# History sums of a chunked delta-rule recurrence: a transfer within SBUF in place of a round trip through DRAM, and another placement of the history products

## The reference, cut to what matters

```python
def step(St, inp):                 # one of 128 steps, for 16 sequences x 16 heads
    kt, qt, vt, at, bt = inp
    Sk = jnp.einsum('bhij,bhj->bhi', St, kt)
    err = Sk - vt
    Sn = at[..., None] * St - (bt[..., None] * err)[..., None] * kt[:, :, None, :]
    ot = jnp.einsum('bhij,bhj->bhi', Sn, qt)
    return (Sn, ot)
```

## Time and profile before

| what | value |
| --- | --- |
| median of 3 runs | 3042.21 us (3035.08 to 3061.76) |
| the profiled execution's own time | 3051.64 us |
| its span | 3050.0 us |
| TensorE, VectorE, ScalarE, GpSimd busy | 68%, 61%, 35%, 39% of the span |
| the recurrence, leaves 0 to 15 | 681.6 to about 1919 us, 1237 us |

### The profile page before, as it was taken

One profiled execution on the slowest core, in us unless ns is written; L12 is line 12 of the kernel. 1 busy time (PEld: TensorE's weight loads), 2 busy tenths in 40 slices (PEclk: granted clock), 3 DMA queues, 4 the chain that ended last, 5 costly groups with the idle time before them and its releaser, 6 DMA issues. The chain is left out here.

```text
span 3050.0 us, 41308 instructions
## 1 busy us (share of the span) xinstructions
PE 2080.3 (68%) x12114; PEld 1426.5 (47%) x12114; DVE 1852.3 (61%) x4462; ACT 1056.3 (35%) x2356; POOL 1183.0 (39%) x1443
## 2 busy tenths in 40 slices
PE   8999999966766666556556446599967553479700
PEld 4555555534555554444345335578733331157600
DVE  5777777767776677776667548545537482023234
ACT  2555555534444444444334234222300100112200
POOL 1444444446443333333333323244444217311175
PEclk8999999987787787787777777799989565579955
DMA  3666666663677788999999993422221602048732
GB/s 93 121 121 121 120 121 121 121 148 71 155 189 176 198 210 222 232 243 240 245 241 251 263 281 82 155 76 76 77 83 33 218 11 71 1 144 264 219 101 84
DMA packets 680751, 457.64 MB, mean 150 GB/s; under 512 B 309583, under 2 KB 625790, under 8 KB 674312
## 3 DMA queue, kind: packets, MB, share of 16 engines
q1 hardware_dynamic: 550891, 314.96, 40.9%
q0 software_dynamic: 50080, 96.70, 11.8%
q10 hardware_dynamic: 79616, 44.06, 5.0%
HBM read 245.54 MB, written 207.77 MB: 149 GB/s over the span
## 5 line engine op out<-in xcount | busy, mean ns | idle before, releaser
L918 ACT ACTIVATE p_diag_o<-p_ident,p_gd 128x128 f32<-128x128 f32 x1152 | 361.7, 389 | 509.2 <-PE p_ps_o L874 483.2
L384 DVE SCALAR_TENSOR_TENSOR p_y<-p_ps_proj,p_w,p_y 128x508 f32<-128x508 f32 (+2 forms) x576 | 416.0, 741 | 115.4 <-ACT p_y L298 101.8
L874 PE MATMUL p_ps_o<-p_ws,p_diag_o 128*128 128x128 f32 x1792 | 327.3, 340 | 128.4 <-DVE p_ws L620 80.0
L726 POOL DMA_DIRECT2D p_near_g<-gram x512 | 284.5, 565 | 289.3 <-PE p_ps_n L847 288.8
L874 PEld LDWEIGHTS p_ps_o<-p_ws,p_diag_o 128*128 128x128 f32 x1792 | 284.0, 240 | 200.6 <-DVE p_ws L620 101.8
L833 PE MATMUL p_ps_z<-p_turned,p_gcol 112*32 112x128 f32 x3584 | 159.6, 319 | 318.3 <-DMA p_turned<-history 318.2
L234 PE MATMUL p_ps_proj<-p_x,p_w 128*128 128x512 f32 x768 | 343.1, 597 | 2.7 <-ACT p_beta_t L289 2.7
L198 POOL TENSOR_TENSOR p_kq<-p_y,p_sig 128x512 f32<-128x512 f32 x128 | 162.2, 1271 | 377.6 <-ACT p_sig L309 376.9
L833 PEld LDWEIGHTS p_ps_z<-p_turned,p_gcol 112*32 112x32 f32 x3584 | 104.7, 126 | 382.4 <-DMA p_turned<-history 343.0
L570 DVE SCALAR_TENSOR_TENSOR p_zo<-p_ws,p_gd,p_zo 128x128 f32<-128x128 f32 x768 | 243.9, 351 | 3.8
L564 DVE TENSOR_TENSOR p_ws<-p_ws,p_dec 128x128 f32<-128x128 f32 (+2 forms) x192 | 119.0, 620 | 205.7 <-PE p_ps_o L874 205.7
(11 more groups left out here) (223 smaller groups left out, 3837.0 us busy)
## 6 DMA issues: line engine op xcount, KB each, us to landing
history<-p_hist SPq DMA_DIRECT2D x18, 2048.0 KB, 14.9
gram<-p_gram SPq DMA_DIRECT2D x64, 512.0 KB, 5.4
history_sums<-p_sums ACTq DMA_DIRECT2D x112, 256.0 KB, 5.5
p_zo<-history_sums SPq DMA_DIRECT2D x28, 1024.0 KB, 8.3
p_wgu<-in_wguT SPq DMA_DIRECT2D x64, 352.0 KB
decays<-p_dec SPq DMA_DIRECT2D x64, 256.0 KB, 2.3
beta_v<-p_bv SPq DMA_DIRECT2D x64, 256.0 KB, 2.5
p_dec<-decays POOLq DMA_DIRECT2D x32, 512.0 KB, 6.5
```

The costliest lines, as they stand in the source:

```text
L384: nc.vector.scalar_tensor_tensor(out=yv[:, :, s:], in0=pv[:, :, 0:T - s], scalar=par[j % 2][:, kind, TAPS - 1 - s:TAPS - s], in1=yv[:, :, ...
L726: pool.dma_start(near_g[h * HALF:(h + 1) * HALF, :, f, h, :], gram_dram[g * BG:(g + 1) * BG, c, c * C:c * C + HALF, h, e0:e0 + HALF] .rear ...
L874: nc.tensor.matmul(ps_o[s // 4 % 2][:, s % 4, :], diag_o[p // DO % NDO][:, p % DO, :], rows[:, r, :], start=(s % 4 == 0 and r == 0), stop= ...
L918: last = nc.scalar.activation(diag_o[n % NDO][:, p % DO, :], ident[:], ACT.Copy, scale=gd[g][:, r, s:s + 1])
```

## The change

- `batch_row` no longer writes to DRAM. It sends the tile `sums` straight to `zo[g]`, in 4 transfers of 64 KB a batch row: the source is one quarter of the tile's row on all 128 partitions, the target 4 partitions (four heads) of `zo[g]` with 16 KB each. All are issued by ScalarE.
- For the first batch row of a leaf ScalarE first waits until `zo[g]` is free: error rows saved, outputs stored, kept rows copied.
- SP's two loads of `zo[g]` and the waits ahead of them are gone, and so is the DRAM tensor.
- VectorE waits at a leaf's start (c > 0) for the semaphores of the 32 transfers (`z_out`) in place of those of the two loads.
- `UNITS_AFTER` has an entry for each of the 16 steps: 0, 0, 0, 0, 1, 1, 2, 4, then 2, 1, 1, 1, 1, 1, 1, 0. The near products stand between steps 7 and 8 with no unit among them.

```diff
--- before.py
+++ after.py
@@ -414,7 +414,7 @@
     clear(nc, used)
 
 
-def recurrence(nc, a_dram, bv_dram, gram_dram, beta_dram, hist_dram, sums_dram, o_dram):
+def recurrence(nc, a_dram, bv_dram, gram_dram, beta_dram, hist_dram, o_dram):
 
     GR = 2
     BG = B // GR
@@ -437,8 +437,8 @@
     NW = 2
     BANKS = 4
     CHAINS = 4
-    UNITS_AFTER = (0, 0, 1, 2, 2, 2, 3, 3)
-    UNITS_NEAR = UNITS - sum(UNITS_AFTER)
+    UNITS_AFTER = (0, 0, 0, 0, 1, 1, 2, 4, 2, 1, 1, 1, 1, 1, 1, 0)
+    assert sum(UNITS_AFTER) == UNITS
     with ExitStack() as ctx:
         m = Pool(nc, ctx)
         hist = [m.sb(f"p2_hist{g}", [P, OLD, DH]) for g in range(GR)]
@@ -491,7 +491,6 @@
         hist_saved = [m.sem(f"p2_hist_saved{g}") for g in range(GR)]
         z_cp = m.sem("p2_z_cp")
         z_out = [m.sem(f"p2_z_out{i}") for i in range(NS)]
-        zo_in = [m.sem(f"p2_zo_in{g}") for g in range(GR)]
         block = ctx.enter_context(nc.Block())
 
         def step_ops(half, k):
@@ -578,7 +577,8 @@
                 dve.wait_ge(gd_in[g], (c + 1) * (BG + 1) * DMA)
                 dve.wait_ge(zo_zero, GR)
                 if c:
-                    dve.wait_ge(zo_in[g], c * (2 * DMA))
+                    for i in range(NS):
+                        dve.wait_ge(z_out[i], (at - GR + 1) * (BG // NS * UB * QUADS * DMA))
 
                 def step(half, k, p_at, w_at, u_at):
 
@@ -762,8 +762,6 @@
             store_o(LEAVES - 1)
             for g in range(GR):
                 pool.wait_ge(o_out[g], DMA * NCHUNK)
-            for i in range(NS):
-                pool.wait_ge(z_out[i], GR * ROUNDS * (BG // NS) * DMA)
 
         @block.sync
         def _(sp):
@@ -808,14 +806,6 @@
                 for u in range(NTURN, UNITS):
                     load_columns(u)
                     load_rows(u, 0, rows)
-                sp.wait_ge(o_out[g], (c + 1) * DMA)
-                if c + 1 < ROUNDS:
-                    sp.wait_ge(kept[g], (c + 1) * 2)
-                for half in range(2):
-                    seqs = slice(half * ZB * H, (half + 1) * ZB * H)
-                    for i in range(NS):
-                        sp.wait_ge(z_out[i], (at * (BG // NS) + (half + 1) * (ZB // NS)) * DMA)
-                    sp.dma_start(zo[g][seqs].rearrange("p f s i -> p (f s) i"), sums_dram[g, seqs]).then_inc(zo_in[g], DMA)
 
         @block.tensor
         def _(pe):
@@ -882,21 +872,17 @@
             for at in range(LEAVES):
                 units = UNITS if 0 < at <= ROUNDS * GR else 0
                 u = 0
-                for s in range(HALF):
+                for s in range(C):
+                    if s == HALF:
+                        pe.wait_ge(near_g_in, (at + 1) * 2 * H * DMA)
+                        near_product(at, 0)
+                        near_turn(at, 0)
+                        near_product(at, 1)
+                        near_turn(at, 1)
                     own_rows(at, s)
                     while u < min(units, sum(UNITS_AFTER[:s + 1])):
                         history(at - 1, u)
                         u += 1
-                pe.wait_ge(near_g_in, (at + 1) * 2 * H * DMA)
-                near_product(at, 0)
-                near_turn(at, 0)
-                near_product(at, 1)
-                while u < units:
-                    history(at - 1, u)
-                    u += 1
-                near_turn(at, 1)
-                for s in range(HALF, C):
-                    own_rows(at, s)
 
         @block.scalar
         def _(act):
@@ -924,12 +910,19 @@
                 k = at * BG + b
                 act.wait_ge(mm_done, (k + 1) * UB)
                 if k >= NS:
-                    act.wait_ge(z_out[k % NS], k // NS * DMA)
+                    act.wait_ge(z_out[k % NS], k // NS * (UB * QUADS * DMA))
                 nc.scalar.copy(sums[k % NS][:], ps_z[k % NZ][:]).then_inc(z_cp, 1)
 
                 act.wait_ge(z_cp, k + 1)
-                act.dma_start(sums_dram[g, b * H:(b + 1) * H].rearrange("(q h) e i -> (h e) q i", h=4),
-                              sums[k % NS][:]).then_inc(z_out[k % NS], DMA)
+                if b == 0:
+                    act.wait_ge(u_saved[g], (at // GR + 1) * 2 * DMA)
+                    act.wait_ge(o_out[g], (at // GR + 1) * DMA)
+                    if at // GR + 1 < ROUNDS:
+                        act.wait_ge(kept[g], (at // GR + 1) * 2)
+                for q in range(UB * QUADS):
+                    p0 = b * H + q * 4
+                    act.dma_start(zo[g][p0:p0 + 4].rearrange("p f s i -> p (f s i)"),
+                                  sums[k % NS][:, q, :]).then_inc(z_out[k % NS], DMA)
 
             def near_rows(at, f):
 
@@ -970,18 +963,14 @@
 
                 if 0 < at <= (ROUNDS - 1) * GR:
                     keep(at - 1)
-                for s in range(HALF):
+                for s in range(C):
+                    if s == HALF:
+                        near_rows(at, 0)
+                        near_rows(at, 1)
                     made = past(s, made)
                     while (b + 1) * UB <= min(units, sum(UNITS_AFTER[:s + 1])):
                         batch_row(at - 1, b)
                         b += 1
-                near_rows(at, 0)
-                near_rows(at, 1)
-                while b * UB < units:
-                    batch_row(at - 1, b)
-                    b += 1
-                for s in range(HALF, C):
-                    made = past(s, made)
         used = m.sems
     clear(nc, used)
 
...
```

2 lines of the change are left out of this document (1 added, 1 removed).

## The result

The changed kernel takes 3342.24 us (median of 4, 3336.33 to 3354.68), the kernel before 3038.64 us in the runs beside it: a ratio of 1.0987 (95% interval 1.0922 to 1.1053). Slower, as forecast, and inside the whole range, which reached to rival A at 3430 us, but by about 300 us where 163 were forecast, and above the forecast's own 3120 to 3300. The profiled execution has a span of 3334.6 us, 284.6 more than before.

A forecast was written before the change was run, and what follows sets the result against it. Early leaves were taken as bound by latency between engines, late ones by DMA engines. Growths of +25, +70, +60 and +8 made +163 on the profiled 3050 us, 3205 us for a median; its own range 3120 to 3300.

The forecast's parts named there:

- rival A: Sums' transfers: few target partitions are a bottleneck of their own; at 1.5 us a transfer +224, 3430 us; chance 0.24.
- four engines a transfer: Sums' transfers to 4 partitions: each carried by the same four DMA engines, 32 packets each, 32 us a leaf.
- the wait at step 5: VectorE's wait for `ws` at step 5, 15.5 us in leaf 12, would go with the first unit behind step 4.
- leaf 15: Last leaf, without sums of its own: would wait 5 to 10 us for the last batch row, +8 us.
- I take 1.0 us: Time of one 64 KB transfer to 4 partitions, near its 32 packets at 30 ns (0.96 us).
- the forecast's own sum: Leaf length, as in leaf 3: 20 us before sums, 32 of sums, 24 of other work, 2 of latency: 78 us.
- the bound from the same rows, 1.5 us: Time of a 64 KB transfer to 4 partitions at half the 8-partition loads' rate of at least 87 GB/s.
- The wait at a leaf's start: VectorE at each leaf's start: a new wait of 5 to 10 us for the last batch row's transfers.
- hidden, at most 124: ScalarE issuing four transfers for one, 0.37 us each: 124 us in all, hidden unless diagonals are late.
- The moved units: Units behind step 4 let VectorE run on to mid-leaf; in leaf 12 that alone would save some 15 us.
- There only 8 units, not 13, stand ahead of the near product: Mid-leaf: fewer units precede the near product, part of the some 15 us saved in leaf 12.
- Rivals B and C: B: transfers spread over 16 engines or rotate, 2956 us, chance 0.20; C: four engines, other packets quicker, 3045 us, 0.12.

The follow-up runs named there:

- probe: Kernel before plus an end stage where ScalarE sends groups of 64 KB transfers within SBUF; a transfer took 1.40 us adjacent, 1.11 two apart, 0.83 four apart.
- spaced: Changed kernel with heads placed otherwise in PSUM, so each transfer goes to 4 partitions four apart, not adjacent; 1.048 times the kernel before.
- stride2: Changed kernel with each transfer's four target partitions two apart, not adjacent; 1.063 times the kernel before.
- quarter: Changed kernel with targets four partitions apart and each transfer moving a quarter of its bytes, so three quarters of the sums are left out; 1.001 times the kernel before.
- mid_order: Kernel before, sums through DRAM, with units after steps 0 to 7 set to 0, 0, 0, 0, 2, 3, 4, 4; 3017.21 us, 0.993 times before.
- no_sums: Changed kernel without the 448 transfers and the waits for them, so history sums never enter; 0.957 times the kernel before.
- new_order: Kernel before, sums through DRAM, with only the units placed as in the change; 1.022 times the kernel before.

## Why the prediction was right or wrong

**Direction right, mechanism right but for the packets' time.** What came as forecast: four engines a transfer (59,136 packets), no gain from leaving DRAM, DMA share down to 0.77 in late leaves with longer leaves, a new wait at the leaf's start, a new wait of ScalarE for its own transfers (77.9 us), the wait at step 5 gone (below), leaf 15 not longer itself (57.5 us, 58.0 before). A landing of the last of four transfers above 6 us: 7.4. What did not: a packet took 43.8 ns, not 30. "Well over 30 ns each on average" was the prediction's own sign for rival A, and it came true beside the forecast's signs.

**The term that was mis-sized: "I take 1.0 us".** It measured 1.40 in the kernel, by the packets' time, and 1.40 in probe, by the clock. The 30 ns were read from transfers over all 128 partitions and taken over to four adjacent ones. They do hold for four that lie apart: spaced has 31 ns and 1.00 us, and lost 4.8%, 146 us of 3042, where the forecast had 163 (spaced's slower products are in its loss too, so the nearness is partly luck). The remaining 0.051 of after's 0.099 came with the adjacent targets (0.036 of it by the cleaner comparison with stride2, whose targets are still two apart). Put into the forecast's own sum, 44.8 us of sums a leaf in place of 32:

| leaves | forecast | with 1.40 us | measured |
| --- | --- | --- | --- |
| leaf 3 | 78 | 20 + 44.8 + 24 + 2 = 91 | 89.0 |
| leaf 8 | 94 | 22 + 44.8 + 38 + 2 = 107 | 106.0 |
| leaf 13 | 108 | 116.3 / 0.96 = 121 | 115.1 |
| 1 to 5, growth | +25 | +91 | +99 |
| 6 to 10, growth | +70 | +135 | +129 |
| 11 to 15, growth | +68 | +122 | +69 |

The growths are differences of L595's starts: leaves 1 to 5 from 353.3 to 452.5 us, 6 to 10 from 395.1 to 524.2, 11 to 15 from 426.9 to 495.9. With the right term the first two come out within 8 us, and all leaves at +348, against +297 measured and +163 forecast. Late leaves do not: there the sum counts other work at before's share, and 8 us for leaf 15 that lie in leaf 14 now. They grow less than early ones, which the form of the sum (a full set of four engines) did not allow for; that they agree with +68 is chance. The reason given for 1.0 was that the 0.8 us of the earlier trace rows hold gaps; the bound from the same rows, 1.5 us, was the nearer one. It was near by luck: its 87 GB/s are of three loads of 8 partitions together, and probe's transfers to 8 adjacent partitions got 58.

**Rival A: right in kind, not in size.** Few adjacent partitions are slow by themselves; at 1.40 us it stayed just under the 1.5 from which it was to decide, and its 3430 us are nearer to 3342 than the forecast's 3205. So the forecast's four engines and A's slow targets acted together, and the forecast had only the first. (A's 48 us a leaf belong to eight batch rows, 32 transfers, not to the four that it names.)

By the figure of the Trainium skill alone (SBUF — State Buffer, "Door 1: The DMA port swizzle", 27.6 GB/s for partitions 0 to 3, 2.4 us for 64 KB) it would have been near +600. In these runs that rate is met only where transfers follow each other to partitions that it puts on one port, as in the fourth group of probe (2.6 us); the kernel's move on, and took 1.40.

**The wait at a leaf's start: 5 to 10 us forecast, 16 measured** (224.0 over 14). The copy came some 4 us after VectorE's last step, as forecast, but the last transfer landed 11.5 us after the first issue. Issuing four took 4.1 of them, and for 3.2 the error rows' stores had the engines.

**ScalarE's issue: 0.37 us each forecast, "hidden, at most 124".** All 448 of after, durations in ns (min/median/max):

```profile
L924 ACTq DMA_DIRECT2D p_zo<-p_sums x448: 557/574/8744, 765.1 to 2151.0; - x150
```

0.57 us, and up to 8.7, which looks like earlier transfers holding it up: in quarter, with a quarter of the bytes, the longest is 1.6. ScalarE is idle 417 us by issue ahead of L904 alone. It was not all hidden, since at mid-leaf `near_rows` stands behind it, 4.2 us in leaf 3; what it costs in all was not separated. That the moved `near_rows` was queued behind two batch rows of after's "4" at step 7 is a step that the prediction did not take.

**The moved units: half right.** In leaf 12 VectorE no longer waits at step 5 (1609.83 in the earlier trace rows); all its waits of that leaf now:

```profile
1825.76 0.23 DVE L595 COPY p_pp<-p_dec 128x128 f32<-128x128 f32 x1 [16.68 <-DMA p_zo<-p_sums]
1881.53 1.47 DVE L566 TENSOR_TENSOR p_zo<-p_zo,p_ps_x 128x512 f32<-128x512 f32 x2 [16.69 <-PE p_ps_x L848]
1887.57 0.43 DVE L563 TENSOR_TENSOR p_ws<-p_ws,p_dec 128x256 f32<-128x256 f32 x1 [2.82 <-PE p_ps_o L864]
1908.95 0.96 DVE L563 TENSOR_TENSOR p_ws<-p_ws,p_dec 128x768 f32<-128x768 f32 x1 [9.58 <-PE p_ps_o L864]
1933.95 0.23 DVE L595 COPY p_pp<-p_dec 128x128 f32<-128x128 f32 x1 [16.87 <-DMA p_zo<-p_sums]
```

In place of the 15.5 us stand a longer wait at mid-leaf (4.6 before, 16.7 now) and waits in the second half's steps (3.7 before, 12.4 now); the 16.7 at the leaf's start come on top. "There only 8 units, not 13, stand ahead of the near product" was true and gave nothing, because those eight still wait for history rows. mid_order and no_sums show this without narrow transfers: 269 and 184 us at mid-leaf.

**Rivals B and C** fell with the four engines. B counted on the moved units too; new_order is 1.022 even with 16 engines a transfer.

## What to carry to other kernels

Price a transfer by what its target reaches, not by its bytes: with four target partitions, this kernel paid 1.40 us for 64 KB adjacent and 1.00 four apart, and either was worse than writing 256 KB to DRAM over all partitions and reading it back (in the new order of the units 1.099 and 1.048 against 1.022). Ask of an on-chip copy how many engines carry it and who else needs those engines, and measure it in a few groups at the end of the kernel before moving work onto it. When units of work are shifted off one wait, follow them to the next one that they stand ahead of: here 164 us left `ws` and 128 came back at mid-leaf.
